# Row sums of the attention weights: from ScalarE's accumulators to a VectorE reduction

## The chip, the cores and the metric

The kernel runs on one core of one Trainium2 chip. The metric is the device time of one execution in microseconds (us). Three runs of the kernel before gave 2787.83, 2788.24 and 2789.91 us; their median is 2788.24 us. The core has five engines that run side by side, each with its own queue in order: TensorE (PE), VectorE (DVE), ScalarE (ACT), GpSimd (POOL) and SyncE (SP, which here issues all DMAs). They meet only at semaphores.

## The reference

The input is 128 graphs of 128 nodes with 384 features, and a 128 x 128 matrix for each graph. Two attention layers with 12 heads of 32 features follow each other, each behind a layer norm and a relu and with a residual:

```python
h = jnp.maximum(_layernorm(x, axis=-1), 0.0)
# layer 0
scores = jnp.einsum('bhqd,bhkd->bhqk', q, k) / jnp.sqrt(HD)
scores = jnp.where(adj_e > 0, scores + beta * adj_e, -9000000000000000.0)
probs = jax.nn.softmax(scores, axis=-1)
x = x + jnp.einsum('bhqk,bhkd->bhqd', probs, v)
h = jnp.maximum(_layernorm(x, axis=-1), 0.0)
# layer 1
a = jnp.einsum('bnhd,bmhd->bhnm', q, k) * SCALE + encoding_bias
a = jnp.where(pad_mask[..., None], -jnp.inf, a)      # rows of all zeros
a = jnp.nan_to_num(jax.nn.softmax(a, axis=-1))
x = x + (jnp.einsum('bhnm,bmhd->bnhd', a, v) @ Wo.T + bo)
```

All is float32. The change concerns the denominator of both softmaxes: for every graph, head and query, the sum of 128 exponentials.

## The kernel before

**Tiling.** Four graphs make a group (32 groups), and a group in one layer is a unit (64 units). A unit's attention is cut into 12 chunks: chunk c holds graph c // 3 of the group and heads 4 (c % 3) to 4 (c % 3) + 3. A chunk is thus 4 heads x 128 queries x 128 keys; queries lie on the 128 partitions, 4 x 128 = 512 elements along each.

**Phases and slots.** Work is laid out in phases of 12 slots. In a phase one unit attends, the next one is projected (q, k and v by PE from float16 parts, q and k then go through ACT, DVE, POOL and DMAs), and a third is normalised. The loop body has two phases, first one in which a layer-0 unit attends, then one in which a layer-1 unit attends, and runs 28 times; thirteen phases before and behind it are written out. Each engine goes through the same slots, and its order within a slot is fixed in the code. There is no scheduler.

**The way of a chunk c** (`chunk(u, c)` is its running number, to which all semaphores count):

- slot c-1: PE makes the scores (L781, `score_bank`, two banks); DVE adds bias or matrix, negates and takes the row minimum, which is the negated maximum (`biased_scores`, L575, tiles `neg` and `neg_max`, two buffers of neg). In layer 1 DVE also reduces neg to `neg_min` (L583), with which it finds rows of zeros.
- slot c: ACT first copies the transposed probabilities of chunk c-1 out of PSUM (L493, `probs_t`), then computes the exponentials of chunk c, one instruction for each of 4 heads (`exponentials`, L479, tile `probs`, two buffers). Each has `accum_out`, so that ACT adds up a row while it computes and then writes the sum to `total`. PE transposes probs (`turn_probs`, L792) as its last work in the slot.
- slot c+1: PE multiplies v with probs_t (L807). If chunk c was the third of a graph, DVE takes the reciprocals of the graph's 12 sums (`inverse_sums`, L620 or L622), and in layer 1 spreads them to `inv_wide`; then come statistics for the norm (`norm_stats`, L603 to L612; POOL goes on with `rstd` L406 and `normed` L413).
- slot c+2: PE transposes the result (layer 0, L846) or inv_wide (layer 1, L852) into `misc_bank`; DVE makes `o_rows` (L676) or `o_norm` (L685) of it. One slot later come the transposes of the norm (L868, the same bank), with ACT's `h_hi` (L516) and DVE's `h_lo` (L700).
- slots c+3 and c+4, layer 1 alone: DVE's `o_hi` (L668), POOL's `o_lo` (L431), PE's output projection (L832) and DVE's `result` (L694).

In slots 1 to 6 ACT copies q and k (L531, L534, tile `qk`), DVE casts them (`part_hi`, L710) and POOL makes the rest (`part_lo`, L420); in slots 8 to 11 DVE takes v (L643). In slot 7 of a layer-1 phase DVE builds the next group's bias (L589 to L594).

Of the kernel before, what the change touches and what calls it, by code (L numbers as in the profile page):

```python
# [31 lines left out]
KC = DIM // P  # L32
# [98 lines left out]
def some(value):  # L131

    return not isinstance(value, int) or value > 0


def unit_of_chunk(p, s):


    if s < 0:
        return p.tail, s + SLOTS  # L140
    if s >= SLOTS:
        return p.look, s - SLOTS
    return p.attend, s


def finished(p, s, lag):

    u, c = unit_of_chunk(p, s - lag)
    if u is None or c % KC != KC - 1:
        return None, 0  # L150
    return u, c // KC


def chunk(u, c):

    return u.n * SLOTS + (c + 1)


def build(nc, x, adj, w0q, b0q, w0k, b0k, w0v, b0v, beta, w1q, w1k, w1v, b1v, w1o, b1o, out):
    weights = (w0q, w0k, w0v, w1q, w1k, w1v, w1o)  # L160
    with ExitStack() as ctx:
# [3 lines left out]
        def sem(name):  # L165
            return ctx.enter_context(nc.semaphore(name))
# [104 lines left out]
        neg_ready = sem("neg_ready")  # L271
        min_done = sem("min_done")
        exp_done = sem("exp_done")
        probs_turned = sem("probs_turned")
        probs_t_ready = sem("probs_t_ready")
        pv_done = sem("pv_done")
# [181 lines left out]
        def _(act):  # L458
# [12 lines left out]
            def exponentials(u, c):  # L471
                n = chunk(u, c)
                act.wait_ge(neg_ready, n)

                if some(n - 2):
                    act.wait_ge(probs_turned, n - 2)
                b, first = c // KC % 2, c % KC * HC
                for h in range(HC):
                    last = act.activation(probs[c % 2][:, h, :], neg[c % 2][:, h, :], ACT.Exp,  # L479
                                          bias=neg_max[:, b, first + h:first + h + 1], scale=-1.0,  # L480
                                          accum_out=total[:, b, first + h:first + h + 1])
                last.then_inc(exp_done, 1)

            def phase(p):
# [56 lines left out]
        def _(dve):  # L541
# [18 lines left out]
            def biased_scores(u, c):  # L560

                n = chunk(u, c)
                b, first = c // KC, c % KC * HC
                if c % KC == 0 and u.layer == 0:
                    dve.wait_ge(bias_ready, u.group + 1)
                if c == 0 and u.layer == 1:
                    dve.wait_ge(adj1_in, u.group * 16 + 16)
                dve.wait_ge(scores_done, n)

                if some(n - 2):  # L570
                    dve.wait_ge(exp_done, n - 2)
                carry()
                bias = (bias0 if u.layer == 0 else adj1)[:, b, :]
                for h in range(HC):
                    last = dve.tensor_tensor_reduce(  # L575
                        out=neg[c % 2][:, h, :], in0=score_bank[c % 2][:, P * h:P * (h + 1)], in1=bias,
                        scale=-1.0, scalar=HUGE, op0=ALU.add, op1=ALU.min,
                        accum_out=neg_max[:, b % 2, first + h:first + h + 1])
                last.then_inc(neg_ready, 1)
                if u.layer == 1:  # L580

                    dve.wait_ge(neg_ready, n)
                    dve.tensor_reduce(neg_min[:, b % 2, first:first + HC], neg[c % 2][:, :, :], AX.X,  # L583
                                      ALU.max).then_inc(min_done, 1)
# [11 lines left out]
            def norm_stats(u, b):  # L596
# [11 lines left out]
                if some(n - 1):  # L608
# [3 lines left out]
                dve.tensor_scalar(shift_var[:, b % 2, 1:2], moments[:, 1:2], EPS, None,  # L612
                                  ALU.add).then_inc(shift_ready, 1)

            def inverse_sums(u, b):

                dve.wait_ge(exp_done, chunk(u, b * KC + KC - 1))
                n = u.group * GROUP + (b + 1)
                if u.layer == 0:
                    dve.reciprocal(inv0[:, b % 2, :], total[:, b % 2, :]).then_inc(inv0_ready, 1)  # L620
                    return
                dve.reciprocal(inv1[:, :], total[:, b % 2, :]).then_inc(inv1_done, 1)  # L622
                dve.wait_ge(min_done, u.group * SLOTS + (b * KC + KC))
                dve.tensor_scalar(alive[:, :], neg_max[:, b % 2, :], 0.0, None, ALU.not_equal).then_inc(alive_done, 1)
                dve.wait_ge(alive_done, n)
                dve.scalar_tensor_tensor(live[:, :], neg_min[:, b % 2, :], 0.0, alive[:, :], ALU.not_equal,
                                         ALU.max).then_inc(live_done, 1)
                dve.wait_ge(live_done, n)
                dve.wait_ge(inv1_done, n)

                if some(n - 1):
                    dve.wait_ge(inv_turned, n - 1)
                dve.tensor_tensor(inv_live[:, :], inv1[:, :], live[:, :], ALU.mult).then_inc(inv_live_done, 1)
                dve.wait_ge(inv_live_done, n)
                dve.tensor_copy(inv_wide[:, :, :],
                                inv_live[:, :].unsqueeze(2).to_broadcast([P, HEADS, HEAD])).then_inc(inv_wide_ready, 1)
# [9 lines left out]
            def phase(p):  # L646

                bias_slot = SLOTS - 1 if p.attend is not None and p.attend.layer == 0 else 7
                for s in range(SLOTS):
# [4 lines left out]
                    u, c = unit_of_chunk(p, s + 1)  # L654
                    if u is not None:
                        biased_scores(u, c)
                    u, b = finished(p, s, 1)
                    if u is not None:
                        inverse_sums(u, b)
# [241 lines left out]
```

## Time and profile before

| what | value |
| --- | --- |
| runs (3) | 2787.83 to 2789.91 us, median 2788.24 |
| span of the profiled execution | 2786.6 us |
| PE, matmuls | 2492.9 us busy, 89% |
| PE, weight loads | 1447.7 us, 52% |
| DVE | 2035.5 us, 73% |
| ACT | 2045.4 us, 73% |
| POOL | 1205.5 us, 43% |
| mean granted clock of PE | 0.985 of full speed |

The profiled execution is one of its own; only its span is given, from the first to the last instruction. Busy time of PE is modelled (an instruction's end overlaps the next one's start), so it is not a measure of how full PE is. "Idle before" in a group of instructions is idle time of the engine just before them, with the work that ended it.

### The profile page before, as it was taken

The numbers are of one execution on the slowest core, as the hardware profiler recorded it, in microseconds if no ns is written. First come the engines' busy times: TensorE is split into PE (matmuls) and PEld (weight loads), VectorE is DVE, ScalarE is ACT, GpSimd is POOL, SyncE is SP. The second block draws the span as 40 slices with busy tenths as digits, with TensorE's granted clock in tenths as the row PEclk, the third lists the DMA queues.
The fourth block names the chain that finished last, engine by engine and source line by source line (L and its number), as shares of the span: only waits on it lengthen the run. The fifth ranks groups of instructions, "written<-read, shape, count | busy, mean of one in ns | idle before, by whom it ended". The sixth has DMA issues, their size and how long they took to land.

```text
span 2786.6 us, 78169 instructions
## 1 busy us (share of the span) xinstructions
PE 2492.9 (89%) x20772; PEld 1447.7 (52%) x20772; DVE 2035.5 (73%) x10864; ACT 2045.4 (73%) x7824; POOL 1205.5 (43%) x1543
## 2 busy tenths in 40 slices
PE   3699999999999999999999999999999999999976
PEld 2355555555555555555555555555555555555543
DVE  3477777777777777777777777777777777777756
ACT  2577777777777777777777777777777777777765
POOL 1344444454444444444444444444444444444431
PEclk8899999999999999999999999999999999999988
DMA  3333333333333333333333333333333333333321
GB/s 118 90 89 87 93 94 87 95 102 86 88 96 86 94 103 86 86 97 87 94 102 88 85 99 86 94 100 89 83 99 88 95 98 90 82 99 91 78 55 45
DMA packets 164279, 251.27 MB, mean 90 GB/s; under 512 B 29776, under 2 KB 114768, under 8 KB 163920
## 3 DMA queue, kind: packets, MB, share of 16 engines
q1 hardware_dynamic: 163920, 248.11, 33.7%
q14 instruction: 332, 2.72, 0.3%
q8 instruction: 27, 0.44, 0.1%
HBM read 71.83 MB, written 25.17 MB: 35 GB/s over the span
## 4 chain that ended last, share of the span: by engine, by line
PE 45%; ACT 17%; DVE 16%; issue 16%; POOL 3%; SPq 1%; ACTq 1%; DVEq 1%; DMA 0%; POOLq 0%
PE job_bank L765 21%; ACT probs L479 12%; PE pt_bank L792 9%; PE o_bank L807 4%; PE misc_bank L832 4%; DVE neg L575 4%; PE score_bank L781 2%; PE misc_bank L846 2%; DVE stats L603 2%; ACT h_hi L516 2%; ACT probs_t L493 2%; PE misc_bank L868 1%; ACT qk L531 1%; DVE h_lo L700 1%; POOL part_lo L420 1%
## 5 line engine op out<-in xcount | busy, mean ns | idle before, releaser
L479 ACT ACTIVATE probs<-neg,neg_max 128x128 f32<-128x128 f32 x3072 | 1185.5, 390 | 9.4 <-DVE neg_max L575 9.4
L493 ACT ACTIVATE probs_t<-pt_bank 128x512 f32<-128x512 f32 x768 | 458.2, 597 | 567.7 <-PE pt_bank L792 516.5
L406 POOL TENSOR_TENSOR rstd<-shift_var,minus_half 128x1 f32<-128x1 f32 x256 | 152.2, 595 | 1020.3 <-DVE shift_var L612 1020.3
L479 ACT ACTIVATION_READ_ACCUMULATOR probs<-neg,neg_max 128x1 f32 x3072 | 583.9, 190 | 0.0
L792 PE MATMUL pt_bank<-ident,probs 128*128 128x128 f32 x3072 | 476.1, 278 | 57.5 <-ACT probs L479 42.9
L420 POOL TENSOR_TENSOR part_lo<-qk,part_hi 128x512 f16<-128x512 f32 x384 | 459.1, 1205 | 115.6 <-DVE part_hi L710 115.6
L792 PEld LDWEIGHTS pt_bank<-ident,probs 128*128 128x128 f32 x3072 | 362.7, 141 | 238.9 <-ACT probs L479 154.8
L765 PE MATMUL job_bank<-h_hi,w_hi 128*128 128x512 f16 x1152 | 441.4, 383 | 43.9 <-ACT qk L531 25.4
L765 PE MATMUL job_bank<-h_lo,w_hi 128*128 128x512 f16 x1152 | 438.5, 381 | 0.0
L765 PE MATMUL job_bank<-h_hi,w_lo 128*128 128x512 f16 x1152 | 438.0, 380 | 0.0
L575 DVE CUSTOM_DVE_ANT_0 neg<-score_bank,bias 128x128 f32<-128x128 f32 x1536 | 352.8, 285 | 103.3 <-issue 98.6
L575 DVE CUSTOM_DVE_ANT_0 neg<-score_bank,adj 128x128 f32<-128x128 f32 x1536 | 352.6, 284 | 40.6 <-issue 33.1
L807 PE MATMUL o_bank<-probs_t,v 128*32 128x128 f32 x6144 | 328.0, 285 | 45.6 <-ACT probs_t L493 31.9
L807 PEld LDWEIGHTS o_bank<-probs_t,v 128*32 128x32 f32 x6144 | 125.1, 108 | 347.1 <-ACT probs_t L493 265.2
L781 PE MATMUL score_bank<-stack 96*128 96x128 f16 x3072 | 298.9, 219 | 4.7 <-DMA stack<-part_lo 4.7
L700 DVE SCALAR_TENSOR_TENSOR h_lo<-misc_bank,h_hi 128x384 f16<-128x384 f32 x256 | 142.4, 556 | 209.5 <-ACT h_hi L516 209.5
L431 POOL TENSOR_TENSOR o_lo<-o_norm,o_hi 128x384 f16<-128x384 f32 x128 | 117.1, 915 | 376.8 <-DVE o_hi L668 376.8
L710 DVE CAST part_hi<-qk 128x512 f16<-128x512 f32 x384 | 193.0, 503 | 111.8 <-ACT qk L531 63.3
L583 DVE TENSOR_REDUCE neg_min<-neg 128x4 f32<-128x512 f32 x384 | 263.4, 686 | 13.3
L765 PE MATMUL job_bank<-w_hi,h_hi 128*128 128x384 f16 x768 | 251.9, 328 | 0.0
L575 DVE DVE_READ_ACCUMULATOR2_ANT neg_max<- 128x1 f32 x3072 | 251.7, 82 | 0.0
L765 PE MATMUL job_bank<-w_hi,h_lo 128*128 128x384 f16 x768 | 250.1, 326 | 0.0
(69 smaller groups left out, 3949.8 us busy)
## 6 DMA issues: line engine op xcount, KB each, us to landing
stack<-part_hi SPq DMA_DIRECT2D x1024, 96.0 KB, 2.2
stack<-part_lo SPq DMA_DIRECT2D x512, 96.0 KB, 2.2
x_norm<-in_x SPq DMA_DIRECT2D x32, 768.0 KB, 4.5
x_res<-in_x SPq DMA_DIRECT2D x32, 768.0 KB, 4.7
out_x<-result SPq DMA_DIRECT2D x128, 192.0 KB, 1.9
adj<-in_adj SPq DMA_DIRECT2D x64, 256.0 KB, 2.9
stack<-in_L_gnn_Wq SPq DMA_DIRECT2D x2, 576.0 KB, 8.1
stack<-in_L_gnn_Wk SPq DMA_DIRECT2D x2, 576.0 KB, 8.9
```

The costliest lines, as they stand in the source:

```text
L406: pool.tensor_tensor(rstd[:, :], shift_var[:, b % 2, 1:2], minus_half[:, :], ALU.pow).then_inc(rstd_done, 1)
L420: pool.tensor_tensor(part_lo[j // KC][:, j % KC, :], qk32[j % 2][:, :], part_hi[j // KC][:, j % KC, :], ALU.subtract).then_inc(part_lo_rea ...
L479: last = act.activation(probs[c % 2][:, h, :], neg[c % 2][:, h, :], ACT.Exp, bias=neg_max[:, b, first + h:first + h + 1], scale=-1.0, accu ...
L493: act.activation(probs_t[c % 2][:, :, :].rearrange("p h q -> p (h q)"), pt_bank[c % 2][:, :], ACT.Copy).then_inc(probs_t_ready, 1)
L575: last = dve.tensor_tensor_reduce(out=neg[c % 2][:, h, :], in0=score_bank[c % 2][:, P * h:P * (h + 1)], in1=bias, scale=-1.0, scalar=HUGE, ...
L583: dve.tensor_reduce(neg_min[:, b % 2, first:first + HC], neg[c % 2][:, :, :], AX.X, ALU.max).then_inc(min_done, 1)
L700: dve.scalar_tensor_tensor(h_lo[u.parity][:, :, P * b:P * (b + 1)], misc_bank[:, 0:DIM].rearrange("p (c n) -> p c n", c=KC), 0.0, h_hi[u.p ...
L710: dve.tensor_copy(part_hi[j // KC][:, j % KC, :], qk32[j % 2][:, :]).then_inc(part_hi_ready, 1)
L765: last = pe.matmul(to, stationary, moving, start=(c == 0 and n == 0), stop=(c == KC - 1 and n == 2))
L781: last = pe.matmul(score_bank[c % 2][:, P * h:P * (h + 1)], q[0:3 * HEAD, h, c % KC, nodes], k[0:3 * HEAD, h, c % KC, nodes], start=True, ...
L792: last = pe.transpose(pt_bank[c % 2][:, P * h:P * (h + 1)], probs[c % 2][:, h, :], ident[:, :])
L807: last = pe.matmul(o_bank[HEAD * h:HEAD * (h + 1), P * (c % KC):P * (c % KC + 1)], v32[u.parity][:, b, f:f + HEAD], probs_t[c % 2][:, h, : ...
```

## The change

ACT's exponentials no longer have `accum_out`. DVE has a new function `sum_probs`, which reduces all four heads of a chunk in one instruction into four columns of `total`. It stands in slot c+1, behind `biased_scores` of chunk c+2 and ahead of `inverse_sums`. A new semaphore `sum_done` tells that it is done: `inverse_sums` waits for it in place of `exp_done`, and ACT's exponentials of a chunk wait for the sum of the chunk two before, which reads the same buffer of `probs`.

```diff
--- before.py
+++ after.py
@@ -271,6 +271,7 @@
         neg_ready = sem("neg_ready")
         min_done = sem("min_done")
         exp_done = sem("exp_done")
+        sum_done = sem("sum_done")
         probs_turned = sem("probs_turned")
         probs_t_ready = sem("probs_t_ready")
         pv_done = sem("pv_done")
@@ -474,11 +475,12 @@
 
                 if some(n - 2):
                     act.wait_ge(probs_turned, n - 2)
+                if some(n - 2):
+                    act.wait_ge(sum_done, n - 2)
                 b, first = c // KC % 2, c % KC * HC
                 for h in range(HC):
                     last = act.activation(probs[c % 2][:, h, :], neg[c % 2][:, h, :], ACT.Exp,
-                                          bias=neg_max[:, b, first + h:first + h + 1], scale=-1.0,
-                                          accum_out=total[:, b, first + h:first + h + 1])
+                                          bias=neg_max[:, b, first + h:first + h + 1], scale=-1.0)
                 last.then_inc(exp_done, 1)
 
             def phase(p):
@@ -612,9 +614,17 @@
                 dve.tensor_scalar(shift_var[:, b % 2, 1:2], moments[:, 1:2], EPS, None,
                                   ALU.add).then_inc(shift_ready, 1)
 
+            def sum_probs(u, c):
+
+                n = chunk(u, c)
+                b, first = c // KC, c % KC * HC
+                dve.wait_ge(exp_done, n)
+                dve.tensor_reduce(total[:, b % 2, first:first + HC], probs[c % 2][:, :, :], AX.X,
+                                  ALU.add).then_inc(sum_done, 1)
+
             def inverse_sums(u, b):
 
-                dve.wait_ge(exp_done, chunk(u, b * KC + KC - 1))
+                dve.wait_ge(sum_done, chunk(u, b * KC + KC - 1))
                 n = u.group * GROUP + (b + 1)
                 if u.layer == 0:
                     dve.reciprocal(inv0[:, b % 2, :], total[:, b % 2, :]).then_inc(inv0_ready, 1)
@@ -654,6 +664,9 @@
                     u, c = unit_of_chunk(p, s + 1)
                     if u is not None:
                         biased_scores(u, c)
+                    u, c = unit_of_chunk(p, s - 1)
+                    if u is not None:
+                        sum_probs(u, c)
                     u, b = finished(p, s, 1)
                     if u is not None:
                         inverse_sums(u, b)
```

On DVE, in slot 7 of a layer-1 phase in the loop, before (ISA with neg and neg_max are the biased scores; the rows from neg_min to v are what follows them):

```order
L575 ISA neg_max 128x1
L575 ISA neg,neg_max<-score_bank,adj 128x128
L575 ISA neg_max 128x1
L583 TENSOR_REDUCE neg_min<-neg 128x4 [waits neg_ready]
L681 REGISTER_ALU
L685 TENSOR_TENSOR o_norm<-misc_bank,o_t 128x384 [waits o_lo_ready,inv_turned,o_taken]
L640 ISA
L642 ISA [waits job_done]
L643 SCALAR_TENSOR_TENSOR v<-job_bank,bv_rows 128x384 [waits pv_done]
```

and now:

```order
L577 ISA neg_max 128x1
L577 ISA neg,neg_max<-score_bank,adj 128x128
L577 ISA neg_max 128x1
L585 TENSOR_REDUCE neg_min<-neg 128x4 [waits neg_ready]
L622 TENSOR_REDUCE total<-probs 128x4 [waits exp_done]
L694 REGISTER_ALU
L698 TENSOR_TENSOR o_norm<-misc_bank,o_t 128x384 [waits o_lo_ready,inv_turned,o_taken]
L650 ISA
L652 ISA [waits job_done]
L653 SCALAR_TENSOR_TENSOR v<-job_bank,bv_rows 128x384 [waits pv_done]
```

The reduction of probs stands between neg_min and o_norm; everything behind it keeps its order.

On DVE two slots later, where a graph ends, before (reciprocal and what makes inv_wide of it, then the statistics):

```order
L575 ISA neg_max 128x1
L583 TENSOR_REDUCE neg_min<-neg 128x4 [waits neg_ready]
L622 RECIPROCAL inv<-total 128x12 [waits exp_done]
L623 REGISTER_ALU
L624 TENSOR_SCALAR alive<-neg_max 128x12 [waits min_done]
L625 REGISTER_ALU
L626 SCALAR_TENSOR_TENSOR live<-neg_min,alive 128x12 [waits alive_done]
L633 TENSOR_TENSOR inv_live<-inv,live 128x12 [waits inv_turned,inv1_done,live_done]
L635 COPY inv_wide<-inv_live 128x384 [waits inv_live_done]
L603 BN_STATS stats<-x_mid 128x6 [waits x_mid_ready]
```

and now:

```order
L577 ISA neg_max 128x1
L585 TENSOR_REDUCE neg_min<-neg 128x4 [waits neg_ready]
L622 TENSOR_REDUCE total<-probs 128x4 [waits exp_done]
L632 RECIPROCAL inv<-total 128x12 [waits sum_done]
L633 REGISTER_ALU
L634 TENSOR_SCALAR alive<-neg_max 128x12 [waits min_done]
L635 REGISTER_ALU
L636 SCALAR_TENSOR_TENSOR live<-neg_min,alive 128x12 [waits alive_done]
L643 TENSOR_TENSOR inv_live<-inv,live 128x12 [waits inv_turned,inv1_done,live_done]
L645 COPY inv_wide<-inv_live 128x384 [waits inv_live_done]
L605 BN_STATS stats<-x_mid 128x6 [waits x_mid_ready]
```

The reciprocal now waits for the instruction just ahead of it.

On ACT, in the loop, a copy to probs_t, the four exponentials of a chunk and the copy of q or k behind them, before:

```order
L493 ACTIVATE probs_t<-pt_bank 128x512 [waits pv_done,probs_turned]
L473 REGISTER_ALU
L479 ACTIVATE probs,total<-neg,neg_max 128x128 [waits probs_turned,neg_ready]
L479 ACTIVATE probs,total<-neg,neg_max 128x128 x3
L513 REGISTER_ALU
L516 ACTIVATE h_hi<-misc_bank 128x3x128 [waits job_done,h_turned]
L523 REGISTER_ALU
L525 REGISTER_ALU [waits job_done]
L531 ACTIVATE qk<-job_bank,bk_cols 128x512 [waits part_lo_ready,part_hi_ready]
```

and now:

```order
L495 ACTIVATE probs_t<-pt_bank 128x512 [waits pv_done,probs_turned]
L474 REGISTER_ALU
L482 ACTIVATE probs<-neg,neg_max 128x128 [waits sum_done,probs_turned,neg_ready]
L482 ACTIVATE probs<-neg,neg_max 128x128 x3
L515 REGISTER_ALU
L518 ACTIVATE h_hi<-misc_bank 128x3x128 [waits job_done,h_turned]
L525 REGISTER_ALU
L527 REGISTER_ALU [waits job_done]
L533 ACTIVATE qk<-job_bank,bk_cols 128x512 [waits part_lo_ready,part_hi_ready]
```

No instruction has moved; total is no longer written, and the first exponential waits for sum_done too.

## Rows read from the trace of the kernel before

**Rows 1.** The page, busy time of each engine, share of span, instructions.

```profile
PE 2492.9 (89%) x20772; PEld 1447.7 (52%) x20772; DVE 2035.5 (73%) x10864; ACT 2045.4 (73%) x7824; POOL 1205.5 (43%) x1543
```

**Rows 2.** Busy time by stretch: a layer-1 phase, a layer-0 phase, the next layer-1.

```profile
core 0: us, PE busy (x) PEld busy (x) DVE busy (x) ACT busy (x) POOL busy (x), PEclk, DMA share, GB/s
1342.60:1385.90 43.30, 39.22 (x334) 23.34 (x334) 37.51 (x184) 32.70 (x125) 17.25 (x22) 1.00 0.35 95
1385.90:1425.90 40.00, 37.72 (x316) 21.49 (x314) 25.66 (x157) 30.77 (x121) 20.44 (x26) 1.00 0.35 90
1425.90:1469.20 43.30, 39.24 (x334) 23.33 (x334) 37.51 (x184) 32.73 (x125) 17.23 (x22) 1.00 0.35 94
```

**Rows 3.** Busy time by stretch, later half of the layer-1 phase.

```profile
1363.46:1384.29 20.83, 18.39 (x167) 11.50 (x164) 20.10 (x97) 15.31 (x59) 9.08 (x11) 1.00 0.43 113
```

**Rows 4.** Chain of waits in the layer-1 phase: start, us, what.

```profile
1367.60 0.55 DVE stats L603
...
1372.83 0.55 DVE o_norm L685
...
1375.33 0.35 DVE o_hi L668
...
1379.06 0.55 DVE stats L603
1380.11 0.57 DVE result L694
...
1382.91 1.14 ACT probs L479 x5
```

**Rows 5.** Waits of DVE in 1342.6 to 1385.9: total, times, longest.

```profile
DVE h_lo L700 <- ACT h_hi L516: 1.8, 3, 0.7
DVE part_hi L710 <- ACT qk L531: 1.7, 2, 1.3
DVE neg L575 <- issue: 0.8, 2, 0.4
```

**Rows 6.** Timeline of ACT, layer-0 phase: start, us, instruction [idle before <-releaser].

```profile
1415.30 0.60 ACT L493 ACTIVATE probs_t<-pt_bank 128x512 f32<-128x512 f32 x1 [0.75 <-PE pt_bank L792]
...
1418.18 0.60 ACT L493 ACTIVATE probs_t<-pt_bank 128x512 f32<-128x512 f32 x1 [0.38 <-PE pt_bank L792]
```

**Rows 7.** Waits of PE's weight loads in 1385.9 to 1425.9.

```profile
PEld pt_bank L792 <- ACT probs L479: 3.0, 5, 0.9
```

**Rows 8.** Groups by line: busy us, mean ns | idle before, releasers.

```profile
L479 ACT ACTIVATE probs<-neg,neg_max 128x128 f32<-128x128 f32 x3072 | 1185.5, 390 | 9.4 <-DVE neg_max L575 9.4
L479 ACT ACTIVATION_READ_ACCUMULATOR probs<-neg,neg_max 128x1 f32 x3072 | 583.9, 190 | 0.0
...
L493 ACT ACTIVATE probs_t<-pt_bank 128x512 f32<-128x512 f32 x768 | 458.2, 597 | 567.7 <-PE pt_bank L792 516.5 <-issue 51.0
...
L583 DVE TENSOR_REDUCE neg_min<-neg 128x4 f32<-128x512 f32 x384 | 263.4, 686 | 13.3
...
L508 ACT ACTIVATE o_t<-o_bank 128x384 f32<-128x384 f32 x256 | 120.6, 471 | 3.9 <-PE misc_bank L832 2.0 <-PE o_bank L807 1.9
```

**Rows 9.** Timeline of ACT, two of four exponentials of a chunk.

```profile
1402.61 0.60 ACT L493 ACTIVATE probs_t<-pt_bank 128x512 f32<-128x512 f32 x1 [1.55 <-PE pt_bank L792]
1403.10 0.39 ACT L479 ACTIVATE probs<-neg,neg_max 128x128 f32<-128x128 f32 x1
1403.39 0.19 ACT L479 ACTIVATION_READ_ACCUMULATOR probs<-neg,neg_max 128x1 f32 x1
1403.48 0.39 ACT L479 ACTIVATE probs<-neg,neg_max 128x128 f32<-128x128 f32 x1
```

**Rows 10.** Timeline of DVE in the layer-1 phase.

```profile
1361.38 0.58 DVE L710 CAST part_hi<-qk 128x512 f16<-128x512 f32 x1 [1.29 <-ACT qk L531]
...
1374.72 0.69 DVE L583 TENSOR_REDUCE neg_min<-neg 128x4 f32<-128x512 f32 x1
1375.33 0.35 DVE L668 CAST o_hi<-o_norm 128x384 f16<-128x384 f32 x1
```

**Rows 11.** Timeline of DVE and PE, first slots of a layer-0 phase.

```profile
1391.40 0.56 DVE L694 SCALAR_TENSOR_TENSOR result<-misc_bank,x_mid_bo 128x384 f32<-128x384 f32 x1
...
1392.32 0.55 PE L852 MATMUL misc_bank<-ident,inv_wide 128*128 128x128 f32 x3
```

**Rows 12.** Busy time by stretch, five late slots of the layer-0 phase.

```profile
1409.78:1424.32 14.54, 13.05 (x122) 7.57 (x120) 9.92 (x66) 12.30 (x50) 8.75 (x12) 1.00 0.42 98
```

**Rows 13.** Timeline of ACT, first exponential behind the bias slot.

```profile
1372.22 0.40 ACT L479 ACTIVATE probs<-neg,neg_max 128x128 f32<-128x128 f32 x1 [0.32 <-DVE neg_max L575]
```

## The prediction

> **What bounds the kernel now.** I read the page's busy shares first: PE is busy 89% of the span, VectorE (DVE) and ScalarE (ACT) 73% each, so a quarter of DVE looks free [rows 1]. That average mixes two kinds of phase, so next come stretches of one phase each. A phase in which layer 1 attends takes 43.3 us and DVE is busy 37.5 us of it; a phase in which layer 0 attends takes 40.0 us with 25.7 us of DVE; the third row shows that the pattern repeats exactly [rows 2]. So the room on DVE is in the layer-0 phases. In the later half of the layer-1 phase there is none: from 1363.46 to 1384.29 DVE is busy 20.10 of 20.83 us [rows 3]. The chain of waits through that half says that DVE is also what the end hangs on: it runs through stats, o_norm, o_hi, stats and result, all on DVE, and goes over to ACT's exponentials only behind result, at 1382.91 [rows 4]. All the idle time of DVE in the layer-1 phase is 1.8 + 1.7 + 0.8 = 4.3 us [rows 5].
>
> In the layer-0 phase PE sets the pace, and in its later six slots a loop between PE and ACT does: transposes of the probabilities, copy to probs_t, four exponentials, transposes again. The copies start at 1415.30 and 1418.18, 2.88 us apart [rows 6]; PE's weight loads wait for the exponentials 5 times there, 3.0 us in all [rows 7].
>
> **The change part by part.** (a) Removed from ACT: 3,072 accumulator reads of 190 ns and the accumulation with them [rows 8]. They overlap the exponential: in rows 9 an exponential starts at 1403.10, its read at 1403.39, the next exponential at 1403.48. What goes is therefore not 0.190 but at least the 0.09 us from the read's start to the next exponential, 4 x 0.095 = 0.38 us for a chunk. That is one end, if the next exponential can start where the read did; below it lies zero, if the reads fill a gap that the exponentials need anyway. The other end comes from copies without accumulator: 597 ns for 512 elements, 471 ns for 384, so 126 ns for 128 elements [rows 8], and about 0.22 us for 128, with starts some 0.1 us closer (from probs_t at 1402.61 to the exponential at 1403.10 [rows 9] are 0.49 of 0.597 us): 0.12 instead of 0.385, or 1.06 us a chunk. I take 0.38, since it is read from the operation itself.
>
> The Trainium skill, "ScalarE: Activation LUTs", section "What ACT_TABLE_LOAD costs", gives about 280 ns + 0.833 ns per element for an ACTIVATE whose bias is a pointer, and an overlap of about 93 ns back to back. For 128 elements that is an estimate of 387 ns, 294 ns from start to start: the trace's 390 ns agree with it, and by it 4 x 0.09 = 0.36 us would go from a chunk.
>
> (b) Added to DVE: one reduction of 512 elements for each of 768 chunks. The same form is there: neg_min takes 686 ns [rows 8]. The next instruction starts earlier, though: one begins at 1374.72 and o_hi at 1375.33, 0.61 us later [rows 10]. On a packed DVE the price is 0.605 us, 465 us in all; by the page of the profile it will read as 527 us of busy time.
>
> The Trainium skill, "VectorE: DVE Perf Modes", section on the TRN2 errata, gives 58 cycles + one per element for SBUF to SBUF and says that the measured fixed term is about 150: estimates of 594 and 690 ns. The trace shows both, 605 as the distance and 686 as the duration; by the larger one the added time of a layer-1 phase would be 8.3 in place of 7.3 us.
>
> (c) Added wait: the reciprocal waits for the sum just before it on its own engine, so the hidden 0.08 us (686 - 605) show, 4 times in a phase: 0.3 us.
>
> (d) Added wait: the exponentials of chunk n wait for the sum of chunk n-2, which stands behind neg (and in layer 1 neg_min) of chunk n on DVE. ACT is now 9.4 us idle for neg in the whole run [rows 8]. In layer 1 the exponential can start 0.61 + 0.69 + about 0.1 = 1.4 us later than neg allows. Behind it in ACT's queue stand o_t, h_hi and the qk copies; PE's transposes of that chunk and the second next scores wait for it. Where ACT starts later than that anyway, the wait is free. I price it at nothing beyond DVE's own lateness, since neg is made a slot ahead; the other end is in the second rival. The sum's own wait for the exponentials of the chunk before the last is free: neg waited for the same ones.
>
> (e) Sum for a layer-1 phase: 12 x 0.605 = 7.3, + 0.3 of (c) = 7.6 us more on DVE. Of the 4.3 us of idle time, 3.64 lie before the packed half. Of those, 1.29 are one wait for qk [rows 10] that DVE causes itself (its part_hi goes to POOL, whose part_lo releases ACT's copy): it moves along when DVE is late, so I don't let it absorb anything. 2.35 absorb, and so does a wait of 0.66 for h_hi at the end of the phase. 7.6 - 3.0 = 4.6 us later. Bounds: all 4.3 absorb, 3.3 us; nothing does, 7.6 us.
>
> (f) Start of a layer-0 phase: result is written at 1391.40 + 0.56 and PE's transposes that need the bank start at 1392.32, 0.36 us later [rows 11]. One sum more goes in front of result: +0.2 us.
>
> (g) The layer-0 phase: before its last six slots the exponentials have slack, nothing moves. In the six slots the loop of 2.88 us falls by 0.38 to 2.50 at best, 6 x 0.38 = 2.3 us (below the 3.0 us that PE waits for them). But DVE between 1409.78 and 1424.32 is busy 9.92 us in five slots [rows 12], 1.98 a slot; with the sum 2.59. DVE thus takes back 0.1 of 0.38 in every slot, and 6 x 0.27 = 1.6; some of it is lost to the reciprocal's wait: 1.5 us gained. Bounds: 0 and 2.3.
>
> Net for a pair of phases: 4.6 + 0.2 - 1.5 = 3.3 us. There are 32 groups, and about 31 pairs in which both layers run beside projections: 102 us. Own span 2786.6 + 102 = 2889; the median of the runs shown is 1.6 us above the span, so 2890 us, 3.7% slower. By this ACT falls to about 1460 us busy at most (2045 - 584), and that buys little: its idle time was no limit in layer 1.
>
> **The rivals.** First, the sums fall into DVE's waits wholly. For it: 27% of DVE are idle, and in early layer-1 slots there is a wait in nearly every slot. Then +3.3 in layer 1 and -2.3 in layer 0: 1.0 us a pair, 31 us, 2819 us. Against it: the chain runs over DVE itself through the packed half.
>
> Second, the gate of (d) decides: DVE's reductions stand between neg and the exponentials, so nothing absorbs and the layer-0 loop gains nothing. 7.6 + 0.2 = 7.8 us a pair, 242 us, 3030 us; half way, 2960. For it: the exponentials at 1372.22, in the slot in which DVE builds a bias first, already wait 0.32 us for neg [rows 13]. Against it: only 9.4 us of such waits in all, and neg is normally ready a slot ahead.
>
> Third, faster: the loop of PE and ACT is the limit in both phases, and takes DVE's load along. The place is the layer-1 half where ACT's exponentials are on the chain [rows 4]; the price is 0.38 for each of about four chunks there, 1.5 us, and 2.3 in layer 0: -3.8 a pair, -118 us, 2670 us if all sums were free. It decides once a layer-1 phase gets less than 1.5 us longer from the sums. The packed half holds six sums, 3.6 us, against 0.73 us of DVE that is not busy, which speaks strongly against it.
>
> That the change does not do what it says I give nothing: the reads are gone from ACT's order and a reduction stands in each slot of DVE's.
>
> **How the numbers follow.** The forecast 0.64, the second rival 0.16, the first 0.14, the third 0.06. The forecast's own range is 2850 to 2935 (net 2.1 to 4.8 us a pair). To leave out no more than 2 in 10, the range goes from 2822, where the first rival begins, to 2965, the middle of the second. A change below 0.2% (5.6 us) is what I count as none: that needs a net of under 0.2 us a pair, the lower end of the first rival, 0.04. Faster is the third rival, 0.06; slower is the rest, 0.90.
>
> **What would show it.** In the profile after: 768 reductions of 686 ns on DVE and its busy time at about 2560 us; ACT's below 1500, and exponentials 0.29 us apart; the layer-1 phase at about 48 us with DVE busy throughout, the layer-0 phase at 38.7; more and longer waits of PE for o_norm, o_lo, result and h_lo; ACT idle before probs_t longer. Wrong would be: ACT waiting for total for hundreds of microseconds (second rival); a layer-1 phase under 47 us (first or third); exponentials still 0.385 us apart ((a) at its lower bound); a layer-0 phase not shorter.

## The result, and the profile after

The changed kernel takes 2950.86 us (median of 5, 2945.33 to 2970.77), the kernel before 2788.24 us (5 runs, 2783.97 to 2789.91). The ratio is 1.0596, with a 95% interval of 1.0566 to 1.0626: 163 us or 6% slower, inside the range of 2822 to 2965 and 61 us above the predicted 2890. The profiled execution is the longest of the five (2970.77 us, span 2968.9), so its numbers lie some 20 us above the median run.

The page's busy times, to be read beside [rows 1]:

```profile
PE 2525.4 (85%) x20772; PEld 1486.0 (50%) x20772; DVE 2513.7 (85%) x11632; ACT 1787.8 (60%) x4752; POOL 1206.6 (41%) x1543
```

DVE has 478 us more, ACT 258 us less, and PE, with the same instructions, 32 us more. (The busy time of an engine counts the overlap of two instructions once, so its sum grows by less than the reductions' 521.0 us.) The groups that answer to [rows 8] (line, operation, names, count | busy, mean ns | idle before and its releaser):

```profile
L482 ACT ACTIVATE probs<-neg,neg_max 128x128 f32<-128x128 f32 x3072 | 973.1, 390 | 74.6 <-DVE total L622 73.5
L495 ACT ACTIVATE probs_t<-pt_bank 128x512 f32<-128x512 f32 x768 | 458.4, 597 | 856.8 <-PE pt_bank L805 856.8
...
L622 DVE TENSOR_REDUCE total<-probs 128x4 f32<-128x512 f32 x768 | 521.0, 678 | 0.5 <-ACT probs L482 0.5
```

The reductions are there, 678 ns each, and hardly ever wait for the exponentials (0.5 us in all). ACT's idle time before probs_t grows from 567.7 to 856.8 us, by more than the 258 us that ACT was relieved of.

Busy time by stretch, as in [rows 2], but from the first biased scores of one layer to the first of the other. First the kernel before, a layer-1 and a layer-0 phase:

```profile
1340.97:1383.10 42.13, 38.46 (x330) 22.61 (x330) 36.96 (x182) 32.52 (x124) 16.73 (x22) 1.00 0.37 103
1383.10:1424.32 41.22, 38.52 (x324) 22.22 (x324) 26.26 (x161) 31.01 (x122) 20.97 (x27) 1.00 0.32 82
```

and the changed kernel, the same two kinds:

```profile
1418.40:1466.60 48.20, 40.21 (x335) 23.73 (x335) 44.08 (x195) 28.83 (x78) 17.42 (x23) 0.96 0.34 93
1466.60:1509.34 42.74, 39.02 (x316) 22.82 (x314) 34.59 (x172) 26.59 (x73) 20.16 (x26) 0.96 0.29 74
```

This layer-1 phase is 6.1 us longer than the one before, with 4.6 forecast, and this layer-0 phase is 1.5 us longer where 1.3 less were forecast. The granted clock is 0.96 in both, but not in all phases. Two others of the changed kernel, a layer-0 and a layer-1 phase:

```profile
1196.15:1237.41 41.26, 37.40 (x316) 22.00 (x314) 34.22 (x171) 26.67 (x73) 20.36 (x26) 1.00 0.30 76
1328.63:1375.65 47.02, 38.48 (x335) 22.97 (x335) 43.99 (x194) 28.81 (x77) 17.42 (x23) 1.00 0.35 95
```

Where the clock stays up, layer 0 takes what it took before and layer 1 is 4.9 us longer. The timeline of DVE shows what happens at the loop's end and start (start us, us, instruction [idle before <-releaser]).

```profile
1468.77 0.55 DVE L653 SCALAR_TENSOR_TENSOR v<-job_bank,bv_rows 128x384 f32<-128x384 f32 x1
1470.80 0.06 DVE L547 MEMSET carrier_v<- 128x1 f32 x1 [1.48 <-issue]
...
1473.04 0.29 DVE L577 CUSTOM_DVE_ANT_0 neg<-score_bank,bias 128x128 f32<-128x128 f32 x1 [1.47 <-issue]
1473.25 0.09 DVE L577 DVE_READ_ACCUMULATOR2_ANT neg_max<- 128x1 f32 x1
1473.25 0.68 DVE L622 TENSOR_REDUCE total<-probs 128x4 f32<-128x512 f32 x1
...
1476.27 0.56 DVE L707 SCALAR_TENSOR_TENSOR result<-misc_bank,x_mid_bo 128x384 f32<-128x384 f32 x1
```

DVE has been packed to the end of the loop body (the first line is its last instruction), then stands still twice without waiting for any engine, 1.48 and 1.47 us, then does the new sum, the reciprocals and the statistics, and only then result. On PE at the same time:

```profile
1474.45 0.43 PE L820 MATMUL o_bank<-probs_t,v 128*32 128x128 f32 x8
1476.96 0.54 PE L865 MATMUL misc_bank<-ident,inv_wide 128*128 128x128 f32 x3 [2.09 <-DVE result L707]
...
1478.46 0.63 PE L778 MATMUL job_bank<-h_hi,w_lo 128*128 128x512 f16 x1
1478.89 1.06 PE L805 MATMUL pt_bank<-ident,probs 128*128 128x128 f32 x4
```

PE waits 2.09 us for result, and a little later every matmul takes longer (0.63 in place of 0.38 us). Busy time by stretch there, the granted clock in the third number from the end:

```profile
1475.00:1477.00 2.00, 0.04 (x1) 0.04 (x1) 1.75 (x11) 0.85 (x3) 0.61 (x2) 1.00 0.00 0
1477.00:1478.50 1.50, 1.50 (x9) 0.86 (x10) 1.50 (x10) 0.00 (x0) 0.78 (x2) 0.95 0.38 131
1478.50:1481.50 3.00, 3.00 (x13) 1.71 (x11) 1.66 (x12) 1.51 (x5) 0.00 (x0) 0.50 0.31 87
```

For 3 us PE is granted 0.50 of its clock, the 1.2 GHz level, while it is busy all the time. In the kernel before the loop holds no such stretch. In the changed one there are 37 between 208 and 2650 us. They lie at or just behind three waits of PE: 16 at this wait for result in a layer-0 phase, 13 behind a wait for o_norm late in a layer-1 phase, 8 behind a wait for qk in its middle. One of each of the last two:

```profile
1184.63 0.75 PE L881 MATMUL misc_bank<-ident,normed 128*128 128x128 f32 x3 [2.08 <-DVE o_norm L698]
...
1439.59 0.39 PE L778 MATMUL job_bank<-h_hi,w_hi 128*128 128x512 f16 x1 [1.62 <-ACT qk L533]
```

What they cost can be read inside this one execution, since the same phase occurs with and without them. Phases between 300 and 2400 us, by what their clock did:

| phases of the changed kernel | number | mean length, us |
| --- | --- | --- |
| layer 0, clock at 1.00 | 10 | 41.26 |
| layer 0, half clock at result | 14 | 42.89 |
| layer 1, clock at 1.00 | 5 | 47.02 |
| layer 1, half clock behind o_norm | 11 | 47.03 |
| layer 1, half clock behind qk | 7 | 48.18 |

So a stretch at half clock costs 1.63 us at result, 1.16 us at qk and nothing behind o_norm, where the layer-1 phase ends as DVE lets it. 16 x 1.63 + 8 x 1.16 is about 35 us of this execution. The wait for result is there in every round between 300 and 2400 us, 2.0 to 2.5 us long, also in those where the clock stays up. The five runs fit: at a mean clock of 0.965 the time is 2945.33 us, at 0.963 and 0.964 2950.69 to 2952.10, at 0.960 2970.77.

The chain of waits (start, us, what) ran through ACT's stall and PE here in the kernel before:

```profile
1384.92 1.60 issue
...
1386.71 0.60 ACT probs_t L493
...
1387.36 0.43 PE o_bank L807 x8
```

Now it is DVE's:

```profile
1469.32 1.25 issue
...
1471.57 1.47 issue
...
1473.34 0.61 DVE total L622
...
1475.08 0.55 DVE stats L605
...
1476.27 0.57 DVE result L707
...
1477.51 1.59 PE job_bank L778 x6
```

### The profile page after: what moved, and what is told of

Its sections match the earlier page's. It is cut to its first block, busy times and chain, and to the rows that moved or that the text cites. A ratio compares the mean times of both kernels' runs of the same rounds, so it can differ in the third digit from the quotient of the medians.

```text
span 2968.9 us, 75921 instructions
## 1 busy us (share of the span) xinstructions
PE 2525.4 (85%) x20772; PEld 1486.0 (50%) x20772; DVE 2513.7 (85%) x11632; ACT 1787.8 (60%) x4752; POOL 1206.6 (41%) x1543
## 4 chain that ended last, share of the span: by engine, by line
DVE 38%; PE 29%; issue 20%; ACT 6%; POOL 3%; DVEq 2%; SPq 1%; DMA 1%; ACTq 0%; POOLq 0%
PE job_bank L778 15%; DVE neg L577 9%; DVE total L622 6%; PE pt_bank L805 5%; DVE neg_min L585 4%; ACT probs L482 4%; DVE stats L605 3%; PE o_bank L820 3%; DVE h_lo L713 2%; DVE part_hi L723 2%; PE misc_bank L845 2%; DVE v L653 2%; PE score_bank L794 1%; PE misc_bank L881 1%; DVE neg_max L577 1%
## 5 line engine op out<-in xcount | busy, mean ns | idle before, releaser
L482 ACT ACTIVATE probs<-neg,neg_max 128x128 f32<-128x128 f32 x3072 | 973.1, 390 | 74.6 <-DVE total L622 73.5
L495 ACT ACTIVATE probs_t<-pt_bank 128x512 f32<-128x512 f32 x768 | 458.4, 597 | 856.8 <-PE pt_bank L805 856.8
L407 POOL TENSOR_TENSOR rstd<-shift_var,minus_half 128x1 f32<-128x1 f32 x256 | 164.2, 641 | 1094.1 <-DVE shift_var L614 1094.1
L778 PE MATMUL job_bank<-h_hi,w_hi 128*128 128x512 f16 x1152 | 452.5, 393 | 107.0 <-DVE h_lo L713 52.8
L622 DVE TENSOR_REDUCE total<-probs 128x4 f32<-128x512 f32 x768 | 521.0, 678 | 0.5 <-ACT probs L482 0.5
L805 PE MATMUL pt_bank<-ident,probs 128*128 128x128 f32 x3072 | 482.7, 281 | 13.8 <-ACT probs L482 4.3
L805 PEld LDWEIGHTS pt_bank<-ident,probs 128*128 128x128 f32 x3072 | 382.7, 145 | 162.6 <-ACT probs L482 63.9
L778 PE MATMUL job_bank<-h_lo,w_hi 128*128 128x512 f16 x1152 | 450.1, 391 | 0.0
L778 PE MATMUL job_bank<-h_hi,w_lo 128*128 128x512 f16 x1152 | 450.0, 391 | 0.0
L723 DVE CAST part_hi<-qk 128x512 f16<-128x512 f32 x384 | 229.9, 599 | 30.7 <-ACT qk L533 27.7
L778 PE MATMUL job_bank<-w_lo,h_hi 128*128 128x384 f16 x768 | 253.7, 330 | 0.0
```

The source lines that it names most:

```text
L407: pool.tensor_tensor(rstd[:, :], shift_var[:, b % 2, 1:2], minus_half[:, :], ALU.pow).then_inc(rstd_done, 1)
L495: act.activation(probs_t[c % 2][:, :, :].rearrange("p h q -> p (h q)"), pt_bank[c % 2][:, :], ACT.Copy).then_inc(probs_t_ready, 1)
L622: dve.tensor_reduce(total[:, b % 2, first:first + HC], probs[c % 2][:, :, :], AX.X, ALU.add).then_inc(sum_done, 1)
L723: dve.tensor_copy(part_hi[j // KC][:, j % KC, :], qk32[j % 2][:, :]).then_inc(part_hi_ready, 1)
L778: last = pe.matmul(to, stationary, moving, start=(c == 0 and n == 0), stop=(c == KC - 1 and n == 2))
L805: last = pe.transpose(pt_bank[c % 2][:, P * h:P * (h + 1)], probs[c % 2][:, h, :], ident[:, :])
```

## The experiments

Theory 1 was: DVE's load sets the pace in layer 1, the relief of ACT helps only in layer 0, and the surplus over the forecast comes from the start of the loop. The rivals were that the gate between sum and exponentials costs, that the relief is worth nothing, and that the cost is spread evenly. All ratios below are against the kernel before, on the same chip.

**ACT's relief alone.** The rows are not added up at all; total is set to 1 once, so normalisation is left out.

```diff
-                                          bias=neg_max[:, b, first + h:first + h + 1], scale=-1.0,
-                                          accum_out=total[:, b, first + h:first + h + 1])
+                                          bias=neg_max[:, b, first + h:first + h + 1], scale=-1.0)
...
+            dve.memset(total[:, :, :], 1.0)
```

> ScalarE's accumulators are gone and nobody adds up the rows (total is set to 1 once, so the weights are not normalised): the relief of ScalarE alone. Theory 1 (VectorE's load costs, ScalarE's relief is worth little in the changed kernel because VectorE takes the pace over): without that load the late half of a layer-0 phase gets 6 x 0.38 us shorter and layer 1 gets about 1 us, 3.3 us a pair, so about 2690 us, range 2670 to 2740. Rival (the exponentials are nowhere the limit, relief is worth nothing): 2780 to 2790 us.

2706.05 us, ratio 0.9713 (0.9697 to 0.9729): 80 us faster, inside theory 1's range. Four exponentials now take 1.26 us, so (1.26 - 0.39) / 3 = 0.29 us from start to start, down from 0.385:

```profile
1299.92 0.60 ACT L492 ACTIVATE probs_t<-pt_bank 128x512 f32<-128x512 f32 x1 [0.37 <-PE pt_bank L792]
1300.41 1.26 ACT L479 ACTIVATE probs<-neg,neg_max 128x128 f32<-128x128 f32 x4
```

**DVE's load alone.** ACT keeps its accumulators, DVE adds up too.

```diff
-                                          bias=neg_max[:, b, first + h:first + h + 1], scale=-1.0)
+                                          bias=neg_max[:, b, first + h:first + h + 1], scale=-1.0,
+                                          accum_out=spare[:, b, first + h:first + h + 1])
```

> VectorE adds up the rows and ScalarE keeps its accumulators, which write to a tile that nobody reads: the load of VectorE and the added waits alone. Theory 1 (VectorE is the pace in layer 1 and nearly so in layer 0): ScalarE's relief is worth little beside it, so 2950 to 3000 us. Rival (the relief is what holds the changed kernel at 2951 us): the full 2.3 us a pair and more come on top, 3020 to 3060 us.

3009.63 us, ratio 1.0802 (1.0784 to 1.0820): 224 us slower. The time lies between the two expected ranges, so neither expectation held. The relief is worth 59 us beside the load (3010 to 2951) and 80 us without it: not little, as theory 1 had it, and less than the rival's 70 and more.

**One layer at a time.** The new form for layer 0 alone, then for layer 1 alone; the other layer keeps its accumulators, and the waits for sum_done count the chunks of the one layer.

```diff
-                    last = act.activation(..., scale=-1.0)
+                    at = dict() if u.layer == 0 else dict(accum_out=total[:, b, first + h:first + h + 1])
+                    last = act.activation(..., scale=-1.0, **at)
...
-                    if u is not None:
+                    if u is not None and u.layer == 0:
                         sum_probs(u, c)
```

> Layer 0 as changed (no accumulators, sums on VectorE), layer 1 as before. Theory 1 (VectorE has room in layer-0 phases): 1.5 us a pair gained, 47 us, so about 2740 us, range 2725 to 2775; PE's clock stays at full speed at the start of the loop. Rival (the added wait of the exponentials for the sums, or the sums ahead of result at the start of the loop, cost in layer 0 too): 2800 to 2850 us.

> Layer 1 as changed, layer 0 as before. Theory 1 (the cost lies in layer-1 phases where VectorE is packed, and in the half clock that PE is granted after its idle time at the start of the loop): 2940 to 3000 us, granted clock below 0.975. Rival (the cost is spread over both layers): 2860 to 2880 us.

Layer 0 alone: 2763.81 us, ratio 0.9920 (0.9903 to 0.9936), **faster than both kernels** by 22 and 187 us, inside theory 1's range. Layer 1 alone: 2919.98 us, ratio 1.0480 (1.0462 to 1.0497), 134 us slower, 20 us below theory 1's range and 40 above the rival's. The loss is mostly layer 1's. But -22 + 134 = 112 us, and both together cost 163: 51 us arise only when both layers carry sums.

Lengths of the phases in us, from the first biased scores of one layer to the first of the other on DVE's timeline, mean of all phases between 300 and 2400 us of the profiled execution (23 to 26 of each kind):

| kernel | layer 0 | layer 1 | pair |
| --- | --- | --- | --- |
| before | 41.33 | 42.12 | 83.45 |
| ACT's relief alone | 39.17 | 41.76 | 80.93 |
| DVE's load alone | 43.94 | 47.05 | 90.99 |
| layer 0 as changed | 40.39 | 42.13 | 82.52 |
| layer 1 as changed | 41.12 | 46.60 | 87.72 |
| changed | 42.21 | 47.38 | 89.59 |
| changed, phases at full clock alone | 41.26 | 47.02 | 88.28 |

With sums in one layer alone no phase loses time to a half clock at result or qk. At full clock both layers together cost 4.83 us a pair, where the two runs of one layer give -0.93 + 4.27 = 3.34. Of the 1.5 us between them 1.1 lie in layer 0: sums there alone save 0.94, sums in layer 1 alone save 0.21, both together save 0.07.

**The start of the loop.** Three edits aim at PE's wait for result and the half clock behind it. The first fills the wait with matmuls that nobody reads:

```diff
+                    if u is not None and s == 1 and u.layer == 1 and p.attend is not None:
+                        for _ in range(FILL):      # 24
+                            pe.matmul(o_bank[:, KC * P:KC * P + P], w_hi[0][:, 0, 0:P], w_hi[0][:, 1, 0:P],
+                                      start=True, stop=True)
```

> The changed kernel with 24 matmuls of 128x128x128 in float16 that nobody reads, in slot 1 of phases whose tail is a layer-1 unit, just ahead of PE's wait for result (2.09 us of idle time there, then some 3.5 us at half the granted clock). Theory 1 (the half clock behind that wait costs): the granted clock stays at 1.00 there and a pair gets up to 1.7 us shorter though PE has 1.3 us more to do, 31 x 1.0 to 1.7, so 2898 to 2925 us. Rival (the half clock falls into time in which PE would wait anyway): 2945 to 2955 us; if the matmuls stand in the way, more.

2938.18 us, ratio 1.0539 (1.0522 to 1.0557), granted clock 0.974: a time between the two expected ranges. With 744 useless matmuls more, the kernel gets 13 us faster, and the stretches at half clock fall from 37 in the middle of the run to 15, all of these late in layer-1 phases, where they cost nothing. The layer-0 phase takes 41.23 us and the layer-1 phase 47.01, the lengths of the changed kernel's phases at full clock. So this run shows the changed kernel without its costly half clock: 13 us less than the median run and, from span to span, 33 us less than the profiled one. What is left, 4.83 us a pair, is 150 us in 31 pairs, and the kernel before plus 150 us is 2938.

The second puts result ahead of the sum on DVE:

```diff
+                    [result's block, unchanged]
                     u, c = unit_of_chunk(p, s - 1)
                     if u is not None:
                         sum_probs(u, c)
...
-                    [result's block, from behind o_norm]
```

> The changed kernel with result ahead of the sum, the reciprocals and the statistics on VectorE. Theory 1 (at the start of the loop PE hangs on result, which stands behind the new sum): PE's wait there falls from 2.09 to about 1 us, the clock stays up, 2890 to 2925 us. Rival (VectorE's total load is all that counts, so order does not): 2945 to 2960 us; if result makes VectorE wait for PE in other slots, more.

2945.54 us, ratio 1.0565 (1.0548 to 1.0583): the interval overlaps the changed kernel's, no gain to be told, as the rival had it. The waits show why. The wait for result is gone, two others are twice as long, and DVE itself, now early at result, waits for PE there:

```profile
ACT probs L482 <- DVE total L622: 152.3, 107, 3.0
PE misc_bank L881 <- DVE o_norm L707: 127.1, 60, 3.0
DVE result L674 <- PE misc_bank L845: 90.2, 101, 4.8
```

in the changed kernel they were

```profile
PE misc_bank L865 <- DVE result L707: 123.9, 84, 2.5
ACT probs L482 <- DVE total L622: 73.5, 54, 2.2
PE misc_bank L881 <- DVE o_norm L698: 62.6, 30, 2.2
DVE result L707 <- PE misc_bank L845: 11.0, 7, 4.1
```

Another order on a packed engine passes the lateness on, and adds waits of its own.

The third lets PE do its last two projection parts of every third slot before the transposes that wait for result, on the changed kernel and, as a control, on the one before:

```diff
+                    if p.project is not None and s % KC == 1:
+                        for part in parts[1:]:
+                            project(p.project, part)
                     u, b = finished(p, s, 2)
...
-                    if p.project is not None:
+                    if p.project is not None and s % KC != 1:
                         for part in parts[1:]:
```

> The changed kernel with PE's last two projection parts of every third slot (slot 1, 4, 7, 10) ahead of the transposes that wait for result. Theory 1 (PE idles there, and its clock falls): the parts fill the wait, 2880 to 2925 us. Rival (VectorE is the pace throughout, o_norm gets later with the transposes): 2950 to 3000 us.

> The kernel before with the order of PE that gained 51 us in the changed kernel. Theory 1 (the gain came from filling PE's waits for result, 123.9 us in the changed kernel and 12.7 us in the kernel before): little or nothing here, 2775 to 2795 us. Rival (the order is simply a better one): 2735 to 2755 us.

On the changed kernel 2899.99 us, ratio 1.0405 (1.0388 to 1.0422), 51 us gained, and the layer-0 phase is down from 42.21 to 39.92 us; none of its 25 phases has a half clock any more. On the kernel before 2780.76 us, ratio 0.9978 (0.9967 to 0.9988), 7 us. Both runs lie in theory 1's ranges. Some six sevenths of the gain are thus the changed kernel's alone, where PE's wait for result falls from 123.9 to 55.6 us; up to 13 of the 51 us are the clock's, by the run with filling matmuls.

**The gate.** Three buffers of probs, so that the exponentials wait for the sum (and for PE's transposes) of the chunk three before.

```diff
-        probs = [sb(f"probs{b}", [P, HC, NODES]) for b in range(2)]
+        probs = [sb(f"probs{b}", [P, HC, NODES]) for b in range(3)]
...
-                    act.wait_ge(probs_turned, n - 2)
...
-                    act.wait_ge(sum_done, n - 2)
...
+                    act.wait_ge(probs_turned, n - 3)
...
+                    act.wait_ge(sum_done, n - 3)
```

> The changed kernel with three buffers of probs, so that the exponentials wait for the sum of the chunk three before. Theory 1 (the added wait of the exponentials is off the path: 73.5 us of ScalarE's idle time for it, while ScalarE waits for the transposes after it anyway): 2935 to 2955 us. Rival (the gate is on the path): 2875 to 2900 us.

2953.54 us, ratio 1.0602 (1.0584 to 1.0620): nothing, inside theory 1's range, although ACT's 73.5 us of waiting for total are gone. The gate is off the path.

**Fewer loop ends.** The body of four phases in place of two, run 14 times, on both kernels.

```diff
-    with eng.Fori(FIRST_LOOP, LAST_LOOP + 1) as i:
-        for p in inside(i):
+    with eng.Fori(FIRST_LOOP // 2, (LAST_LOOP + 1) // 2) as i:
+        for p in inside(i * 2) + inside(i * 2 + 1):
```

> The changed kernel with a loop body of four phases, run 14 times, in place of two phases, 28 times: half the loop ends are gone and no work is moved. Theory 1 (part (f) of the prediction was mis-sized: in the changed kernel VectorE is on the path through the end of the loop, with its two instruction stalls of 1.25 and 1.47 us, PE's wait for result and the half clock behind it): each end costs 3 to 4 us, 14 of them 42 to 56 us, so 2895 to 2910 us. Rival (the stalls belong to fetching instructions wherever it happens, or something else in layer 0 costs): 2935 to 2955 us.

> The kernel before with the same loop body of four phases. Theory 1: there ScalarE's stall of 1.6 us is on the path through the end of the loop and VectorE's of 2.3 us is hidden, so an end costs 1 to 1.6 us, 14 of them 14 to 22 us: 2766 to 2774 us, clearly less than what the changed kernel gains. Rival (an end costs the same in both kernels, so it explains nothing of the difference): it gains as much as the changed kernel.

Both expectations failed. The changed kernel: 2931.16 us, ratio 1.0517 (1.0500 to 1.0535), 20 us faster than with the short body. The kernel before: 2835.70 us, ratio 1.0172 (1.0155 to 1.0189), 48 us slower. The edit is not the clean one it was meant to be: with the long body PE itself stalls once in each round (waits of PE in the kernel before with the long body: total, times, longest):

```profile
PE score_bank L781 <- issue: 45.1, 13, 3.8
```

and an instruction queue that moved 27 packets now moves 198 (name: packets, us that they took, share):

```profile
q8 instruction: 198, 3.24, 0.5%
```

Behind these stalls the clock is halved as well (0.50 from 1408 to 1414 us).

The totals therefore say nothing on theory 1, but the phases do, since every second layer-0 phase of the long body has no loop end in it. The kernel before, a layer-0 phase with a loop end and one without:

```profile
1403.35:1449.37 46.02, 40.88 (x324) 22.99 (x324) 26.37 (x160) 31.12 (x122) 20.99 (x27) 0.93 0.30 76
1491.49:1531.85 40.36, 38.45 (x324) 22.26 (x324) 26.29 (x160) 31.02 (x122) 21.00 (x27) 1.00 0.32 81
```

and the changed kernel, one without, and the layer-1 phase that follows it:

```profile
1363.25:1402.25 39.00, 37.34 (x316) 22.04 (x314) 34.12 (x172) 26.58 (x73) 20.31 (x26) 1.00 0.31 79
1402.25:1448.90 46.65, 39.92 (x335) 23.82 (x335) 44.12 (x195) 28.84 (x78) 17.39 (x23) 0.96 0.37 97
```

Means over 12 phases are 40.36 and 39.01 us without a loop end. Against them a loop end of the short body costs the kernel before 41.33 - 40.36 = 0.97 us. It costs the changed kernel, at full clock, 41.26 - 39.01 = 2.25 us in layer 0 and 47.02 - 46.65 = 0.37 us in the layer-1 phase behind it, 2.62 us together. The changed kernel thus pays 1.65 us more for each loop end. With the half clock at result an end costs it 42.21 - 39.01 + 0.37 = 3.6 us. Theory 1 had given an end 3 to 4 us there and 1 to 1.6 us in the kernel before, so its sizes hold for the short body; what failed is the edit. Without a loop end its layer-0 phase is 1.35 us shorter than before.

**The version pointed to.** Sums on DVE in layer 0, PE's parts ahead, the long body.

> Sums on VectorE in layer 0 alone, PE's two parts ahead of the transposes, and the loop body of four phases: the version the runs point to. Theory 1: 22 us from layer 0, 14 to 22 us from the loop ends, 0 to 10 us from the order, so 2730 to 2752 us. Rival (the gains fall on the same idle time): 2755 to 2765 us.

2812.48 us, ratio 1.0093 (1.0076 to 1.0110): the long body spoils it, and both expectations missed, since they were written before its cost was known. Beside the kernel before with the long body (2835.70) it is 23 us faster. The best kernel run that computes the whole result is thus layer 0 alone with the short body, 2763.81 us. That kernel with PE's parts ahead and the short body was not run.

## Why the prediction was right, and what it missed

**What bounds it.** Right: DVE's late layer-1 half was packed [rows 3], so DVE's idle 27% were of no use there. A layer-1 phase got 4.5 us longer with sums in layer 1 alone, and 4.9 us at full clock in the changed kernel, where (e) said 4.6. My "all the idle time" of 4.3 us was not all: the stretch has 43.30 - 37.51 = 5.8 us [rows 2], 1.5 us of them in short gaps that the view of the waits does not list. The sum of (e) came out without them.

**(a)** 0.38 us a chunk: right, 4 x (0.385 - 0.29). From the figures of the Trainium skill, "ScalarE: Activation LUTs", section "What ACT_TABLE_LOAD costs", the estimate was 0.294 us from start to start, and the trace agrees with 0.29. Wrong was ACT's busy time: I took off the whole 584 us of the reads, and it fell by 258, because a read begins inside its own exponential and the next exponential inside the read [rows 9].

**(b)** 0.605 us on a packed DVE: right. In the changed kernel one reduction starts at 1467.44 and o_hi at 1468.04, another at 1477.60 and o_norm at 1478.20. Of the two estimates from the Trainium skill's page "VectorE: DVE Perf Modes", section on the TRN2 errata, 594 ns is thus the one that a packed queue pays, and 690 ns the duration in the profile (678 here). DVE's busy time came to 2513.7 us where I wrote 2560, for the same reason as ACT's: I added up durations that overlap.

**(c)** The reciprocal starts 0.72 us after the sum ahead of it (1473.25 to 1473.97), so its wait shows 0.12 us where I said 0.08. It was not tried by itself.

**(d)** The gate costs nothing: shown by the third buffer.

**(g)** The relief of a layer-0 phase is 2.16 us without load on DVE, where its upper bound was 2.3; a third of that lies before the eighth chunk, where I had let nothing move. With the load, and away from the loop's end, 1.35 are left of it where I said 1.5.

**(f)** is the step that was mis-sized: +0.2 us for the start of the layer-0 phase, where the runs with the long body give 1.65 us at full clock. I had seen that result left PE only 0.36 us [rows 11]. I had not seen that DVE's own stall at the loop's end, 2.28 us and off the chain behind ACT's 1.79 in the kernel before, comes onto the path as soon as DVE is the last to arrive there; nor that a second stall of 1.47 us follows it. Layer 1's lateness and layer 0's first sum meet at this place, which is why each layer alone is cheap there. That this stall, and not DVE's load at that place, is what the 1.65 us consist of is the reading of the chain, and no run took the stall away by itself.

**The clock** was in no step and no rival. It takes some 35 us of the profiled execution and 13 of the median run. It belongs to (f) for the larger part, behind PE's wait for result, and to the layer-1 phase for the rest, behind the wait for qk.

**The sum.** At full clock a pair came to 4.5 (layer 1) - 1.35 (layer 0) + 1.65 (loop end) = 4.8 us, and 3.3 were forecast. The difference of 1.5 us is 47 us in 31 pairs, and with 13 us of clock that is the 61 us above the forecast.

**What was luck.** The measured time is above the forecast's own range of 2850 to 2935. It lies in the stated range because that reached half way to the second rival, whose mechanism, the gate, had no part in it. One sign that I had named as speaking against me came true as well: the layer-0 phase is not shorter, 42.21 us after 41.33. The step behind that sign was (f), and (g) held.

**The rivals.** The first (DVE's waits take the sums) is refuted by 4.5 us in layer 1 alone, the second (the gate) by the third buffer. The third (faster through ACT's relief) is right in mechanism where there is no load: 80 us; its condition, under 1.5 us of cost in a layer-1 phase, fails by 3. In layer 0 alone both conditions hold, and there the change does gain.

## What to carry to other kernels

Before work is moved to an engine with a quarter of its time free, look at it phase by phase: here the free time lay in one kind of phase, and moving the work there alone turned 6% slower into 0.8% faster. Where an engine becomes the last to arrive at a loop's end, look up its own stall at the branch, which was off the path before, and what waits behind it: here an end cost 0.97 us before and 2.62 after. A wait that was cured by reordering the packed engine came back elsewhere; giving the waiting engine other work to do kept its gain (51 us against 5). A trace that holds the same phase many times, with and without a disturbance, prices it without a further run.

## What the runs showed that I had not expected

- After PE's waits of 1.6 to 2.5 us the granted clock fell in 37 places to 0.50 for some 3 us while PE was busy, though not after each such wait. What it cost depended on who set the pace: 1.63 us at the start of layer 0, 1.16 in the middle of layer 1, nothing late in layer 1, where DVE was the limit. 744 useless matmuls at one of these waits made the kernel 13 us faster.
- A loop body twice as long makes the kernel before 48 us slower, though its layer-0 phases without a loop end are 0.97 us shorter: PE stalls up to 3.8 us in each round, with 198 packets in an instruction queue in place of 27.
- DVE's instruction stall at the loop's start is one of 2.28 us in the kernel before and two of 1.48 and 1.47 us in the changed one, which has only 24 reductions more in the body. Why it splits stays open.
